# A graph network's attention layers: GpSimd's mask products of 1024 columns cut into two of 512

## The reference

```python
# third layer: adding the log before softmax is multiplying the exponentials by the clipped adjacency
logits = einsum('bhqd,bhkd->bhqk', q, k) / sqrt(32) + log(clip(adj, 1e-8, None))[:, None]
x = layer_norm(x + (softmax(logits) @ v) @ Wo.T + bo)
# fourth layer: the same with exp(2*adj - 1) * (0.25 + 0.75*adj) as the factor
weights = softmax(logits + (2*adj - 1)) * (0.25 + 0.75*adj)
weights = weights / weights.sum(-1)
x = x + (weights @ v) @ Wo + bo;  x = x + gelu(ln(x) @ Wf1 + bf1) @ Wf2 + bf2
```

## Time and profile before

| | |
|---|---|
| median of 3 runs | 4708.6 us (4702.09 to 4715.1) |
| the profiled execution | 4708.0 us, span 4706.2 us |
| PE busy | 4119.6 us, 88% |
| DVE busy | 3435.8 us, 73% |
| POOL busy | 2161.7 us, 46% |
| ACT busy | 2023.0 us, 43% |
| mean granted clock of TensorE | 0.94 |

### The profile page before, as it was taken

One profiled execution on the slowest core, in us unless ns is written; L12 is line 12 of the kernel. 1 busy time (PEld: TensorE's weight loads), 2 busy tenths in 40 slices (PEclk: granted clock), 3 DMA queues, 4 the chain that ended last, 5 costly groups with the idle time before them and its releaser, 6 DMA issues.

```text
span 4706.2 us, 67689 instructions
## 1 busy us (share of the span) xinstructions
PE 4119.6 (88%) x20528; PEld 2175.4 (46%) x20528; DVE 3435.8 (73%) x4594; ACT 2023.0 (43%) x3638; POOL 2161.7 (46%) x1192
## 2 busy tenths in 40 slices
PE   7988899888998889988899888998989989899798
PEld 5534365343753337433374333743347433464334
DVE  3798747986479864898658985588855888458893
ACT  3264532644335443354423644235442354424553
POOL 1184702756027560275603755047550466404663
PEclk9998999989989899998999999999999999999999
DMA  3201102011020110201111011110111101111010
GB/s 106 68 19 33 50 24 59 19 32 50 28 57 17 35 48 28 57 17 35 48 33 54 15 37 48 35 50 14 37 48 37 48 14 37 50 36 48 13 38 16
DMA packets 109068, 180.41 MB, mean 38 GB/s; under 512 B 28256, under 2 KB 51040, under 8 KB 108704
## 3 DMA queue, kind: packets, MB, share of 16 engines
q1 hardware_dynamic: 108704, 175.89, 13.0%
HBM read 83.12 MB, written 8.39 MB: 19 GB/s over the span
## 4 chain that ended last, share of the span: by engine, by line
PE 38%; POOL 28%; issue 23%; DVE 7%; ACT 2%; POOLq 1%; DMA 0%; SPq 0%; DVEq 0%; ACTq 0%
POOL region_p L1329 23%; PE ps L514 11%; PE ps L560 9%; PE ps L506 8%; PE ps L712 5%; PE ps L550 2%; DVE row_max L1068 2%; POOL y L1378 1%; POOL rstd L1341 1%; PE ps L601 1%; PE ps L623 1%; POOL v_head L1323 1%; POOL y_t L1394 1%; ACT region_p L832 1%; DVE sums_t L1039 1%
## 5 line engine op out<-in xcount | busy, mean ns | idle before, releaser
L1329 POOL TENSOR_TENSOR region_p<-region_p,mask 128x1024 f32<-128x1024 f32 x640 | 1681.6, 2641 | 384.9 <-ACT region_p L832 384.1
L832 ACT ACTIVATE region_p<-ps 128x512 f32<-128x512 f32 x2048 | 1111.7, 595 | 806.3 <-PE ps L585 804.6
L1068 DVE TENSOR_REDUCE row_max<-ps 128x1 f32<-128x1024 f32 x1024 | 1201.9, 1212 | 67.4 <-PE ps L601 66.4
L623 PE MATMUL ps<-region_p,v_head 128*64 128x512 f32 x4096 | 1079.3, 607 | 140.8 <-POOL region_p L1329 131.7
L1060 DVE TENSOR_TENSOR region_p<-region_p,mask 128x1024 f32<-128x1024 f32 x384 | 725.4, 1889 | 43.1 <-ACT region_p L832 41.0
L601 PE MATMUL ps<-region_k,region_q 96*64 96x512 bf16 x4096 | 668.3, 414 | 99.7 <-DVE row_max L1068 96.4
L585 PE MATMUL ps<-region_q,region_k 97*64 97x512 bf16 x4096 | 665.5, 398 | 1.1
L1341 POOL TENSOR_TENSOR rstd<-var_eps,minus_half 128x2 f32<-128x2 f32 (+1 forms) x160 | 116.6, 729 | 895.9 <-DVE var_eps L1020 895.9
L601 PEld LDWEIGHTS ps<-region_k,region_q 96*64 96x64 bf16 x4096 | 204.8, 114 | 660.8 <-DVE row_max L1068 409.2
L560 PE MATMUL ps<-values,region_k 128*128 128x256 f32 x2048 | 466.8, 383 | 0.0
L623 PEld LDWEIGHTS ps<-region_p,v_head 128*64 128x64 f32 x4096 | 278.8, 138 | 369.2 <-POOL region_p L1329 201.7
(11 more groups left out here) (148 smaller groups left out, 4459.2 us busy)
## 6 DMA issues: line engine op xcount, KB each, us to landing
mask<-in_adj SPq DMA_DIRECT2D x64, 512.0 KB, 7.3
mask<-in_adj_t SPq DMA_DIRECT2D x64, 512.0 KB, 3.5
y_t<-o_raw SPq DMA_DIRECT2D x256, 64.0 KB, 2.0
sums_t<-o_raw SPq DMA_DIRECT2D x256, 64.0 KB, 2.0
region_q<-region_p SPq DMA_DIRECT2D x192, 64.0 KB, 2.0
region_k<-region_p SPq DMA_DIRECT2D x192, 64.0 KB, 2.0
region_q<-sums_t SPq DMA_DIRECT2D x192, 64.0 KB, 2.0
region_k<-sums_t SPq DMA_DIRECT2D x192, 64.0 KB, 2.0
```

What stands on the lines that cost most here:

```text
L623: last = nc.tensor.matmul(ps[64 * c:64 * c + 64, 6 + i, :], v_head[i][:, t, :], probs[:, t % RING, c * HALF:(c + 1) * HALF], start=(t == 0 ...
L832: nc.scalar.activation(probs[:, t % RING, c * HALF:(c + 1) * HALF], ps[:, 4 + c, :], ACT.Exp, scale=DK ** -0.5).then_inc(exp_done, 1)
L1068: nc.vector.tensor_reduce(row_max[i][:, t:t + 1], flat[:, (t % 2) * N:(t % 2 + 1) * N], AX.X, ALU.max)\
L1329: nc.gpsimd.tensor_tensor(p, p, mask[:, t, :], ALU.mult).then_inc(masked_pool, 1)
```

## The change

Each of GpSimd's products is made in two instructions of 512 columns. The first waits for the exponential of the first half alone, the second for that of the second half. Only the second counts on `masked_pool`, so TensorE waits for the same event as before. VectorE's products, the copy of the values and all else stay.

```diff
             def head(b, layer, h, i, last=False):
                 for t in POOL_TILES:
-                    pool.wait_ge(exp_done, att(b, layer, h, 2 * T, 2 * t + 2))
-                    p = probs[:, t % RING, :]
-                    nc.gpsimd.tensor_tensor(p, p, mask[:, t, :], ALU.mult).then_inc(masked_pool, 1)
+                    for c in range(2):
+                        cut = slice(c * HALF, (c + 1) * HALF)
+                        pool.wait_ge(exp_done, att(b, layer, h, 2 * T, 2 * t + c + 1))
+                        p = probs[:, t % RING, cut]
+                        half = nc.gpsimd.tensor_tensor(p, p, mask[:, t, cut], ALU.mult)
+                    half.then_inc(masked_pool, 1)
                     if t == POOL_TILES[1] and not last:
                         copy_values(b, layer, ahead(h), 1 - i)
```

## The result

The changed kernel takes 4758.65 us (median of 4, 4753.29 to 4764.96) against 4711.85 for the kernel before (median of 4): ratio 1.0106, 95% interval 1.0089 to 1.0124. It is slower by 1.1%, 47 us; 4747 and +38 were forecast.

A forecast was written before the change was run, and what follows sets the result against it. GpSimd and VectorE, excluding each other in products, were taken to bound heads 1 to 5. Layer terms of +3.1 (eight fourth) and +1.7 (eight third) sum to 38 us, giving 4747 us; range 4700 to 4800 for 8 in 10.

The forecast's parts named there:

- What bounds the kernel: Heads 1 to 5: VectorE and GpSimd exclude each other in products; the pair is 98% full in a 15.2 us head.
- The floor: Least time of a head in any order: GpSimd's work plus 0.99 per VectorE product; 14.9 us whole, 15.53 in halves.
- The step of a half: GpSimd's halves follow each other after 1.22 us, so a product costs 2.44 instead of 2.31, +0.13.
- The early release: First half's wait: a product ends 0.36 us earlier where GpSimd idled for an exponential; no gain where GpSimd is the bound.
- The -0.35 in head 0: Head 0 of a layer has gaps; its last product starts 0.49 us earlier, so the head shortens by 0.35.
- VectorE's standing: VectorE waits at most 1.27 us instead of 2.36, saving up to about 1.1 at product and cast; the floor is unmoved.
- The ends: Heads 6 and 7: +1.3 us in fourth layers; no change in third, GpSimd needing 33.7 to 35.7, middle 34.7.
- The sum: Over the layers: 8 x 3.1 + 8 x 1.7 = 38 us slower, 4747 us in all, +0.8%.
- 8 that had been added for gaps: In every layer, +0.5 us added for gaps that stay beside the floor.
- The range of the forecast alone: Whole kernel: 4720 to 4785 us, for steps of 1.20 to 1.25 with gaps of 0 to 1.
- The cost of the second instruction: Rival, GpSimd's halves: this cost is hidden, a half steps by 1.155, total 4674 us; chance of faster 0.12.
- The reading that counts VectorE alone: Within the faster rival (0.12): only VectorE counts in heads 1 to 5, TensorE's 0.76 goes, -61 us, 4648.

The follow-up runs named there:

- e6: Kernel before, GpSimd's products whole, with VectorE's three products a head replaced by a one-operand row maximum (tiles unmasked): 4540.0 us, ratio 0.9635.
- e1: Changed kernel with both halves waiting for the exponential of the whole tile: 4770.1 us, ratio 1.0121 to the kernel before.
- e2: Changed kernel with each product in four instructions of 256 columns, two behind each half's exponential: 4930.9 us, ratio 1.0473 to the kernel before.
- e5: Changed kernel (halves) with GpSimd given four tiles (0, 2, 4, 6) instead of five: 4678.6 us, ratio 0.9925 to the kernel before.
- e12: Four GpSimd tiles in halves, tile 0 alone waiting for the whole tile's exponential: 4600.7 us, ratio 0.9763 to the kernel before.
- e4: Kernel before with one of GpSimd's five tiles moved to VectorE, products whole: 4613.0 us, ratio 0.9794.
- e7: VectorE's products replaced by a one-operand row maximum, GpSimd's products in halves: 4628.9 us, ratio 0.9818 to the kernel before.
- e8: VectorE's products replaced by a one-operand maximum, GpSimd's in halves, each product waiting for GpSimd's previous one: 4590.3 us, ratio 0.9741 to the kernel before.

## Why the prediction was right

**What bounds the kernel.** Right. The pair of engines was nearly full: once the exclusion is taken away (e6) a head falls from 15.18 to 14.40, TensorE's time that had been read off as 15.20 - 0.76. The floor held in every kernel with five tiles: 15.53 with halves was computed and 15.58 measured. With the measured step of 1.227, and the measured 0.98 for a product of VectorE (0.99 was read off), it is 12.27 + 0.36 + 2.95 = 15.58. With quarters it is 16.98, and 17.01 was measured.

**The step of a half.** 1.22 was taken between bounds of 1.155 and 1.27; 1.227 was measured (median of the 695 undisturbed pairs). The part that does not shrink is 0.14 us, under the 0.17 to 0.22 that had been read off. Ten halves make the missing 0.007 into 0.07 a head, which is what heads 1 to 5 took above the forecast (+0.40 for +0.33).

**The early release.** Worthless in a full GpSimd, as said (e1). The -0.35 in head 0 is the term that had the wrong sign: head 0 took -0.09 and +0.50. Its length goes with TensorE's clock, whose mean grant in these stretches is 0.74 to 0.83, and which fell differently on the two kernels, so they have to be compared at equal clock. In the fourth layers (the last one aside) head 0 takes 16.47 to 16.48 before and 16.88 to 16.90 after where 0.82 or 0.83 was granted, and 17.2 before and 17.4 after at 0.75 to 0.76. The -0.09 of the third layers is the clock: five of eight had 0.82 in the changed kernel, none before. So head 0 became longer, by 0.2 to 0.4 in the fourth layers. Why is not shown.

**VectorE's standing.** Half right. Its product took at most 2.34 and 1.61 on average, its idle time grew, and TensorE's waits went over to GpSimd's products, 131.7 to 199.2 us of idle at L623. But the cast, for which "as much" was to be saved, stood in the same 96 of 128 cases as before, for 1.2 us instead of 1.1. (With quarters, e2, all 128 take 0.17.) That cost nothing in a head bound by the floor. In a kernel whose heads are above their floor (e5) the cast's stand goes with the loss of all that halves could give.

**The ends.** Fourth layers +1.41 for +1.3. Third layers +0.94 for -0.1: the middle between 9 and 11 of VectorE's turns was taken for no change, and the measured +0.94, set against -1.1 to +0.9, is its upper end. In the changed kernel GpSimd has no gap in heads 6 and 7, and eleven of its halves are stretched by a VectorE instruction in every third layer, seven in every fourth. The same sum gives both: 20 x 1.227 + 0.36 + 11 x 0.98 = 35.7 (35.73 measured), and with 7 it is 31.8 (31.80).

**The sum.** 54 us in the layers for 38: +0.07 x 80 = 6 from heads 1 to 5, 9 from the ends, 9 from head 0, less 8 that had been added for gaps and did not come as such. The total is thus closer than its parts: the 8 cancelled nearly half of what the ends and head 0 were short, and the medians (+47) happen to lie 10 us nearer to the forecast than the profiled executions (+57). This much is luck; the forecast of heads 1 to 5, the largest term, is not. The range of the forecast alone was added up a little narrow: steps of 1.20 to 1.25 with gaps of 0 to 1 give 4717 to 4789, not 4720 to 4785.

**The rivals.** The cost of the second instruction isn't hidden: quarters settle it with 0.14 us an instruction. The reading that counts VectorE alone (4648) is refuted for this division of tiles.

## What to carry to other kernels

Where two engines exclude each other, add the time in which either holds the way, over both, and compare that with the period before looking at either one's idle time: idle time that ends with another engine's semaphore may be the partner's turn. Splitting an instruction shortens the partner's wait but adds its fixed part to that sum (0.14 us here), so it loses when the sum is the bound; moving one tile of five to the engine that is twice as fast lowered the sum and gave 2.1%. When two kernels are compared in a stretch where the clock is not full, compare stretches with the same granted clock. Where a head takes longer than that sum, a small instruction of the partner can matter more than a long one: look at which of them a finer cut or an earlier release lets the other engine get in ahead of (e5 and e12 differ in one wait and by 1.7%).

The version to keep is e4 or e12: 4613.0 and 4600.7 us, ratios whose intervals overlap, 2.1% and 2.4% faster than the kernel before. They weren't timed side by side, so halves aren't shown to help there, and e12 keeps its cast ahead by only 0.11 us.

## What the runs showed of the hardware that was not expected

An engine that stands isn't always let in after the instruction that it meets. VectorE's product stood through seven further halves of GpSimd, 9.99 us (e7), with no instruction of GpSimd stretched: seven of them take 8.65, a step of 1.23. GpSimd had made eleven instructions without a break before it (ten halves and the copy). Once GpSimd waited for its own completion between products, VectorE came in at the first chance in all layers (e8). In kernels where VectorE interrupts often, among them the changed one, it got in after one half each time (no product over 2.34 us); there it met GpSimd after at most four instructions without a break, and after at most eight in e2. But in e7's first layer it came in at once, after eleven as well, so the length of the run alone doesn't decide it. The Trainium skill (GPSIMD Engine Reference, 2.1) says that GpSimd's cores each go on to the next instruction as soon as their own share is done; cores drifted apart would leave no moment in which all are between two instructions, which fits these numbers, but the drift itself was not measured.
